# A recurrent graph stage: the next groups' x copied a round ahead, and the tail of a round moved over other slots

## The reference, cut to what matters

```python
A = (adj != 0).astype(x.dtype)
h = x
for l in range(weight.shape[0]):
    m = jnp.einsum('bnd,de->bne', h, weight[l])
    agg = jnp.einsum('bij,bid->bjd', A, m)
    h = _gru_cell(agg, h, w_ih, w_hh, b_ih, b_hh)
return h * mask[..., None]
...
x = _layernorm(x + _L2_gnn_ref(x, adj, nodemask, ...), axis=-1)
```

## Time and profile before

| | |
|---|---|
| median of 3 runs | 1141.59 us (1139.44 to 1142.74) |
| the profiled execution | 1139.14 us, span 1137.3 us |
| mean granted TensorE clock | 0.967 of full speed |
| TensorE matmuls | 998.3 us busy, 88% of the span |
| VectorE | 901.4 us, 79% |
| ScalarE | 770.9 us, 68% |
| GpSimd | 725.5 us, 64% |
| chain that ended last | TensorE 57%, VectorE 19%, ScalarE 9% |

### The profile page before, as it was taken

The page is one execution under the profiler, slowest core; times in us unless marked ns, Lnnn a source line. Parts: engine busy times, 40 slices in busy tenths (PEclk is TensorE's granted clock), DMA queues, the critical chain, the costliest instruction groups (busy, mean ns, idle before and its releaser), DMA issues.

```text
span 1137.3 us, 21302 instructions
## 1 busy us (share of the span) xinstructions
PE 998.3 (88%) x6138; PEld 602.2 (53%) x6138; DVE 901.4 (79%) x2511; ACT 770.9 (68%) x1311; POOL 725.5 (64%) x751
## 2 busy tenths in 40 slices
PE   3699998495989998998998999899899999958884
PEld 2599998242344544454454454445445445547663
DVE  4599999373679878977977987897797798778996
ACT  1388887473667777776776777777677677726664
POOL 0589898293458657656855865765685685565553
PEclk9699999698999999999999999999999999979997
DMA  6133331234443432333333233242333333303323
GB/s 164 54 105 107 106 110 52 61 64 67 52 71 62 74 75 46 79 60 65 74 64 73 56 74 74 46 83 55 65 80 59 74 56 59 64 11 82 89 75 82
DMA packets 261150, 81.59 MB, mean 72 GB/s; under 512 B 188499, under 2 KB 260972, under 8 KB 261100
## 3 DMA queue, kind: packets, MB, share of 16 engines
q1 hardware_dynamic: 247274, 80.15, 32.3%
q10 hardware_dynamic: 13826, 0.85, 0.9%
HBM read 28.58 MB, written 8.81 MB: 33 GB/s over the span
## 4 chain that ended last, share of the span: by engine, by line
PE 57%; DVE 19%; ACT 9%; issue 7%; POOL 3%; ACTq 2%; DMA 1%; DVEq 0%; SPq 0%; POOLq 0%
PE psum L1198 15%; PE psum L1193 15%; PE psum L1194 15%; PE psum L1222 6%; DVE st L816 4%; DVE x L827 2%; PE psum L1281 2%; ACT psum L727 2%; DVE mv L820 2%; ACT rt L749 2%; DVE ws L963 2%; ACTq L703 2%; PE psum L1236 2%; DVE ot L1105 2%; PE psum L1296 1%
## 5 line engine op out<-in xcount | busy, mean ns | idle before, releaser
L587 POOL TENSOR_TENSOR zh<-zw,ht 128x512 f32<-128x512 f32 x160 | 203.6, 1272 | 102.5 <-ACT zw L752 80.6
L560 POOL TENSOR_TENSOR htp<-ht,htp 128x512 f16<-128x512 f32 x128 | 149.1, 1165 | 117.2 <-ACT htp L738 117.2
L1193 PE MATMUL psum<-htp,wh_hi 128*128 128x512 f16 x480 | 182.6, 380 | 39.3 <-ACT rt L749 24.9
L1193 PE MATMUL psum<-pth,wx_hi 128*128 128x512 f16 x480 | 183.3, 382 | 13.8 <-ACT pth L712 13.6
L1198 PE MATMUL psum<-ptl,wx_hi 128*128 128x512 f16 x480 | 183.3, 382 | 4.1 <-DVE ptl L1012 3.2
L1194 PE MATMUL psum<-pth,wx_lo 128*128 128x512 f16 x480 | 183.2, 382 | 0.0
L1198 PE MATMUL psum<-htp,wh_hi 128*128 128x512 f16 x480 | 182.4, 380 | 0.0
L1194 PE MATMUL psum<-htp,wh_lo 128*128 128x512 f16 x480 | 182.4, 380 | 0.0
L752 ACT ACTIVATE zw<-psum,brz,unscale 128x512 f32<-128x512 f32 x160 | 124.4, 777 | 67.2 <-PE psum L1198 67.2
L993 DVE SCALAR_TENSOR_TENSOR rt<-psum,bhn,rt 128x512 f32<-128x512 f32 x160 | 119.6, 748 | 57.8 <-ACT rt L749 55.7
L712 ACT ACTIVATE pth<-psum 128x512 f16<-128x512 f32 x160 | 95.6, 597 | 93.1 <-PE psum L1222 77.3
(11 more groups left out here) (162 smaller groups left out, 1844.4 us busy)
## 6 DMA issues: line engine op xcount, KB each, us to landing
adj<-in_adj_dram SPq DMA_DIRECT2D x32, 256.0 KB, 2.9
x<-in_x_dram SPq DMA_DIRECT2D x32, 256.0 KB, 3.3
adjr<-in_adj_dram SPq DMA_DIRECT2D x32, 256.0 KB, 3.0
out_dram<-yo SPq DMA_DIRECT2D x8, 768.0 KB
hnp<-htp SPq DMA_TRANSPOSE x128, 3.1
out_dram<-xq SPq DMA_DIRECT2D x32, 50.0 KB
v<-in_L_gnn_W_dram SPq DMA_DIRECT2D x2, 640.0 KB, 5.3
x3q<-x SPq DMA_DIRECT2D x16, 50.0 KB
```

The costliest lines, as they stand in the source:

```text
L560: nc.gpsimd.tensor_tensor(HT_LO[s % 2], HT[s][:, :], HT_HI[s % 2], ALU.subtract).then_inc(b_htl, 1)
L587: nc.gpsimd.tensor_tensor(ZH[s % 2][:, :], ZW[s % 2][:, :], HT[s][:, :], ALU.mult).then_inc(b_zh, 1)
L1193: mm(dst, w_h[:, col:col + P], h[:, :], start=start, stop=False)
```

## The change

- **x pair.** For l = 0 each stream has a buffer of its own for the pair (`X_OF`): s = 0 and 1 two new ones (`HXP`), made 16 and 15 slots ahead by ScalarE and VectorE (slots 4, 5 and 5, 6 of the round before), s = 2 and 3 the buffers `HNP`, made at lags -1 and 0. ScalarE's copy moves behind `HT_HI` and waits for P matmuls of long before instead of N matmuls. The waits for `b_hn` and `b_h0` move to SyncE, ahead of the transposing DMA.
- **A16** moves from lag 0 to lag -2, and its place in VectorE's slot from before q to after q and the low half of x. The loads of adj for s = 2 and 3 are issued a slot earlier.
- **The tail.** Residual add from lag 6 to 9, behind ZH in GpSimd's slot; `bn_stats` from 7 to 10; `bn_aggr` from 8 to 13; `rstd` from 9 to 15; normalisation from 11 to two halves at 16 and 20. On VectorE all of these move from the end of the slot to between A16 and t1.
- **TensorE.** The fp32 transposes move from before Z to between Z and N.
- Stage B begins 16 slots early and ends at lag 20 instead of 11; slots without an item are empty.

```diff
--- before.py
+++ after.py
@@ -52,6 +52,7 @@
...
     TURN = STREAMS * L
+    EARLY, LAST_LAG = 16, 20
     GC = 16
@@ -178,8 +179,9 @@
...
         HNP = [sb(f"hnp{p}", [P, 2 * G4 * D], F16, scope=sbb) for p in range(2)]
+        HXP = [sb(f"hxp{p}", [P, 2 * G4 * D], F16, scope=sbb) for p in range(2)]
         HT_HI, HT_LO = [t[:, 0:G4 * N] for t in HTP], [t[:, G4 * N:2 * G4 * N] for t in HTP]
-        HN_HI, HN_LO = [t[:, 0:G4 * D] for t in HNP], [t[:, G4 * D:2 * G4 * D] for t in HNP]
+        X_OF = [HXP[0], HXP[1], HNP[0], HNP[1]]
         PT_HI = [sb(f"pth{p}", [P, G4 * N], F16, scope=sbb) for p in range(2)]
@@ -301,14 +303,14 @@
...
                     slot(lambda lag: item(j - lag, it))
-            body(0, range(TURN))
+            body(0, range(-EARLY, TURN))
             if unrolled:
...
                     body(it, range(TURN))
-            body(ROUNDS - 1, range(TURN + 11))
+            body(ROUNDS - 1, range(TURN + LAST_LAG))

@@ -334,6 +336,11 @@
...
                 eng.wait_ge(signal, value)
+
+        def halves(t):
+
+            w = G4 * D
+            return t[:, 0:w], t[:, w:2 * w]

@@ -444,20 +451,23 @@
...
             def slot_b(at):
+                x = at(-1)
+                if x and x[0] == 0 and x[1] < 2:
+                    sp.wait_ge(b_a16, gth(x))
+                    load_b(x[1] + 2, x[2])
                 x = at(0)
...
                 p = s % 2
-                if l == 0 and s < 2:
-                    sp.wait_ge(b_a16, gth(x))
-                    load_b(s + 2, it)
                 if l == 2 and s < 2 and not (isinstance(it, int) and it == ROUNDS - 1):
...
                     sp.wait_ge(b_sxl, gth(x))
-                    sp.dma_start_transpose(blocks(HTP[p]), HNP[p][:, :]).then_inc(b_tr[p], 16)
+                    reach(sp, b_hn, nth(x) - 2)
+                    reach(sp, b_h0, gth(x) - 2)
+                    sp.dma_start_transpose(blocks(HTP[p]), X_OF[s][:, :]).then_inc(b_tr[p], 16)
                 else:
@@ -558,11 +568,6 @@
...
                     nc.gpsimd.tensor_tensor(HT_LO[s % 2], HT[s][:, :], HT_HI[s % 2], ALU.subtract).then_inc(b_htl, 1)
-                x = at(6)
-                if x and x[0] == L - 1:
-                    l, s, it = x
-                    wait_apart(pool, b_ym, gth(x))
-                    nc.gpsimd.tensor_tensor(YB[s][:, :], YB[s][:, :], of_group(x2, x), ALU.add).then_inc(b_y, 1)
                 x = at(1)
@@ -588,6 +593,11 @@
...
                 x = at(9)
+                if x and x[0] == L - 1:
+                    l, s, it = x
+                    wait_apart(pool, b_ym, gth(x))
+                    nc.gpsimd.tensor_tensor(YB[s][:, :], YB[s][:, :], of_group(x2, x), ALU.add).then_inc(b_y, 1)
+                x = at(15)
                 if x and x[0] == L - 1:
@@ -710,14 +720,6 @@
...
                     nc.scalar.activation(PT_HI[s % 2][:, :], P_B, ACT.Copy, scale=UP_P / UP_H).then_inc(b_ph, 1)
-                x = at(0)
-                if x and x[0] == 0:
-                    l, s, it = x
-                    reach(act, b_hn, nth(x) - 2)
-                    reach(act, b_tr[s % 2], turned(x) - 16)
-                    if s >= 2:
-                        act.wait_ge(b_h0, gth(x) - 2)
-                    nc.scalar.activation(HN_HI[s % 2], of_group(x2, x), ACT.Copy, scale=UP_H).then_inc(b_sxh, 1)
                 x = at(3)
@@ -736,6 +738,13 @@
...
                     nc.scalar.activation(HT_HI[s % 2], HT[s][:, :], ACT.Copy).then_inc(b_hth, 1)
+                for lag, some in ((-16, (0, 1)), (-1, (2, 3))):
+                    x = at(lag)
+                    if x and x[0] == 0 and x[1] in some:
+                        l, s, it = x
+                        reach(act, b_at, nth(x) - (TURN if s < 2 else STREAMS))
+                        nc.scalar.activation(halves(X_OF[s])[0], of_group(x2, x), ACT.Copy, scale=UP_H)\
+                          .then_inc(b_sxh, 1)
                 x = at(4)
@@ -971,20 +980,53 @@
...
             def slot_b(at):
-                x = at(0)
+                x = at(4)
+                if x:
+                    l, s, it = x
+                    dve.wait_ge(b_z, nth(x))
+                    dve.wait_ge(b_n, nth(x))
+                    nc.vector.scalar_tensor_tensor(C_B, ZW[s % 2][:, :], 1.0, C_B, ALU.subtract, ALU.mult)\
+                      .then_inc(b_q, 1)
+                for lag, some in ((-15, (0, 1)), (0, (2, 3))):
+                    x = at(lag)
+                    if x and x[0] == 0 and x[1] in some:
+                        l, s, it = x
+                        hi, lo = halves(X_OF[s])
+                        dve.wait_ge(b_sxh, gth(x))
+                        nc.vector.scalar_tensor_tensor(lo, of_group(x2, x), UP_H, hi, ALU.mult, ALU.subtract)\
+                          .then_inc(b_sxl, 1)
+                x = at(-2)
                 if x and x[0] == 0:
...
                       .then_inc(b_a16, 1)
-                x = at(4)
-                if x:
-                    l, s, it = x
-                    dve.wait_ge(b_z, nth(x))
-                    dve.wait_ge(b_n, nth(x))
-                    nc.vector.scalar_tensor_tensor(C_B, ZW[s % 2][:, :], 1.0, C_B, ALU.subtract, ALU.mult)\
-                      .then_inc(b_q, 1)
+                x = at(13)
+                if x and x[0] == L - 1:
+                    l, s, it = x
+                    wait_apart(dve, b_bs, gth(x))
+                    for i in range(G4):
+                        last = nc.vector.bn_aggr(MVB[s][:, 2 * i:2 * i + 2], STB[s][:, 6 * i:6 * i + 6])
+                    last.then_inc(b_mv, 1)
+                x = at(10)
+                if x and x[0] == L - 1:
+                    l, s, it = x
+                    wait_apart(dve, b_y, gth(x))
+                    for i in range(G4):
+                        last = nc.vector.bn_stats(STB[s][:, 6 * i:6 * i + 6], cols(YB[s], i))
+                    last.then_inc(b_bs, 1)
+                for lag, some in ((16, (0, 1)), (20, (2, 3))):
+                    x = at(lag)
+                    if x and x[0] == L - 1:
+                        l, s, it = x
+                        wait_apart(dve, b_rs, gth(x))
+                        for i in some:
+                            last = nc.vector.tensor_scalar(
+                                x2[:, bass.ds(it * (STREAMS * G4 * D) + (s * G4 + i) * D, D)], cols(YB[s], i),
+                                MVB[s][:, 2 * i:2 * i + 1], RSB[s][:, i:i + 1], ALU.subtract, ALU.mult)
+                        if lag == 20:
+                            last.then_inc(b_x3, 1)
                 x = at(3)
@@ -1011,35 +1053,6 @@
...
                                                    ALU.mult, ALU.subtract).then_inc(b_pl, 1)
-                x = at(8)
-                if x and x[0] == L - 1:
-                    l, s, it = x
-                    wait_apart(dve, b_bs, gth(x))
-                    for i in range(G4):
-                        last = nc.vector.bn_aggr(MVB[s][:, 2 * i:2 * i + 2], STB[s][:, 6 * i:6 * i + 6])
-                    last.then_inc(b_mv, 1)
-                x = at(0)
-                if x and x[0] == 0:
-                    l, s, it = x
-                    dve.wait_ge(b_sxh, gth(x))
-                    nc.vector.scalar_tensor_tensor(HN_LO[s % 2], of_group(x2, x), UP_H, HN_HI[s % 2],
-                                                   ALU.mult, ALU.subtract).then_inc(b_sxl, 1)
-                x = at(7)
-                if x and x[0] == L - 1:
-                    l, s, it = x
-                    wait_apart(dve, b_y, gth(x))
-                    for i in range(G4):
-                        last = nc.vector.bn_stats(STB[s][:, 6 * i:6 * i + 6], cols(YB[s], i))
-                    last.then_inc(b_bs, 1)
-                x = at(11)
-                if x and x[0] == L - 1:
-                    l, s, it = x
-                    wait_apart(dve, b_rs, gth(x))
-                    for i in range(G4):
-                        last = nc.vector.tensor_scalar(
-                            x2[:, bass.ds(it * (STREAMS * G4 * D) + (s * G4 + i) * D, D)], cols(YB[s], i),
-                            MVB[s][:, 2 * i:2 * i + 1], RSB[s][:, i:i + 1], ALU.subtract, ALU.mult)
-                    last.then_inc(b_x3, 1)
             run_b(dve, slot_b)
@@ -1217,7 +1230,7 @@
...
                     reach(pe, b_pl, n - 1)
-                    for h, half in enumerate((HN_HI[p], HN_LO[p])):
+                    for h, half in enumerate(halves(X_OF[s] if l == 0 else HNP[p])):
                         for i in range(G4):
@@ -1227,6 +1240,11 @@
...
                     support(0)
+                if x:
+                    g = l * GATE
+                    reach(pe, b_z, n - 1)
+                    hi_passes(Z_B, wh_hi, wh_lo, P, HT_HI[p], True)
+                    lo_pass(Z_B, wh_hi, P, HT_LO[p], False)
                 y = at(4)
@@ -1236,10 +1254,6 @@
...
                 if x:
-                    g = l * GATE
-                    reach(pe, b_z, n - 1)
```

(19 more changed lines are left out.)

1 line of the change is left out of this document (removed).

## The result

The changed kernel takes 1488.38 us (median of 4 runs, 1487.35 to 1488.54) where the kernel before took 1141.37: a ratio of 1.304, 95% interval [1.302, 1.306]. The forecast of the direction and its mechanism held. The time, 1416, was 72 us too low, and the range ended at 1470.

What follows compares the result with a forecast made beforehand. It took a plain slot, 4.33 us, to be bound by TensorE. 118 + 112 + 39 - 5 + 5 + 5 = 274 us on 1139.1 made 1413, with 2.5 for the median 1416; range 1375 to 1470.

Steps and rivals of the forecast that it cites:

- Direction and mechanism: Slower, chance 0.94: VectorE's steps moved ahead of T1 wait for their inputs and delay T1, which TensorE waits for.
- The three waits: On VectorE: statistics on GpSimd's add, normalisation on the inverse deviation, 28 times some 4 us each; A16 on P matmuls, 2.5.
- Statistics: Slots 6 to 9: VectorE waits for GpSimd's residual add behind ZH; 28 slots grow by 4.2 us, 118 us.
- Normalisation: Slots 12 to 15: VectorE waits for the inverse deviation behind ZH; 28 slots grow by 4.0 us, 112 us.
- Change of round: Slots 18 to 3: A16's wait for P matmuls and the moved transposes cost 12.7 us each; net 39 us more.
- A16 held by GpSimd: Slots 18, 19, 0 and 1: A16 also stands while ZH runs on GpSimd; 39 us with it, 10 without.
- Low half of x: On VectorE, moved before T1: costs nothing, as its input is a slot old and idle time covers it.
- The rest: X copies in slots 4 and 5, 3 us; normalisations beside HT_LO in slots 16 and 17, 2; start 1; end 4.
- Relief: Change of round: ScalarE's wait for the N matmuls goes, 5.06 us a round at most.
- rival (3): Each of 56 long waits lowers TensorE's clock for seven matmuls, 1.5 us each, 84 in all: 1500; chance 0.12.

Runs made afterwards that it cites:

- e1: The changed kernel with the residual add at lag 8 and the inverse deviation at lag 14, one slot earlier each; 1214.09 us.
- e2: The changed kernel with A16 at lag -1 instead of -2, nothing else; 1415.35 us.
- e10: The changed kernel with A16 still at lag -2, but at the end of VectorE's slot, behind PT_LO; 1416.41 us.
- e11: The changed kernel with all its lags, but statistics, aggregation and normalisation at the end of VectorE's slot, behind PT_LO; 1200.80 us.
- e3: The changed kernel with residual add at lag 8, inverse deviation at lag 14 and A16 at lag -1; 1150.51 us.
- e4: The changed kernel with 12 more matmuls, result unused, on TensorE between Z and N in slots 6 to 9 and 12 to 15; 1417.13 us.
- e8: e3 with statistics, aggregation and normalisation at the end of VectorE's slot, behind PT_LO; 1119.43 us.
- e9: The kernel before with the x pair's change (high halves at lags -10, -2; low -8, 0), transposes behind Z, normalisation at lag 12; 1110.64 us.
- e5: The kernel before with the x pair's part of the change alone; A16, tail and transposes as before; 1121.23 us.

## Why the prediction was wrong, point by point

- **Direction and mechanism**: right. The three waits are the three longest of VectorE, 28 times in the rounds each, and e1, e2, e10 and e11 take them away one by one. Undoing both kinds (e3) gives back 338 of the 347 us that the change cost.
- **Statistics**, 118 us: at full clock (e4) slots 6 to 9 take 8.1 + 3 x 8.47 = 33.5 us, 4.05 each above plain, 113 in all. Right. The first is 0.4 shorter because its ZH starts at +0.68 instead of +1.06.
- **Normalisation**, 112: 33.7 in e4, 4.09 each, 115 in all. Right.
- **Change of round**, 12.7 each: in e4 slots 18 and 19 take 14.3 - 8.7 = 5.6 us above plain ones (forecast 6.0), and slots 0 to 3 take 23.7 - 17.3 = 6.4 (forecast 6.7): 12.0. Right.
- **A16 held by GpSimd**: right. It took 1.31 us and ended 0.27 us behind ZH.
- **Low half of x**, costed at nothing as its input is a slot old: wrong, though small here. In the changed kernel the two early ones take 1.12 us instead of 0.69, and in e8 slot 6, with no other new step ahead of t1, is 0.29 us longer than a plain one. Beside GpSimd's HT_LO for its whole length it takes 1.62 us (e9). The Trainium skill's page "SBUF — State Buffer", section "SBUF: two separate sides", names beside the two-port mode also a VectorE instruction with two SBUF inputs as bound by the shared ports, against a GpSimd one that reads SBUF. The trace of e9 agrees: the low half reads two SBUF tiles, and it took 1.62 us beside HT_LO, which reads two as well.
- **The rest**: slots 4 and 5, with the x copies on ScalarE, cost 1.1 us a round instead of 0.4. Two normalisations beside HT_LO in slots 16 and 17 cost 0.9 us a round at full clock (e4), 6 us in all instead of 2. The start is 1.5 us later and the last stage 4.0 us longer, as forecast. That the filled kernel, at 1417.13, meets the forecast of 1416 so closely is in part luck: these small errors, of 3 to 5 us each, go both ways.
- **Relief**, 5.06 us a round at most: 3.9 seen in e5, 4.9 in e10. The new place of the transposes and SyncE's two waits had no run of their own; e10 has both, and its 4.9 leaves 0.2 us a round for them.
- **The clock**: here the prediction failed. The mechanism stood there as rival (3), with its price of 1.5 us for each wait, and it came true: in slots 7 to 9 and 12 to 15 of all seven rounds, in slot 6 of rounds 1 and 7 and in slot 18 of rounds 1 to 6. These are 57 stretches, 1.25 us each, 71 us. The step that failed is the choice of value: between a pause of 0.9 us that kept full clock and one of 6.8 that lost it, a pause of 3.3 was given no cost in the sum and 0.12 of the chances, and the range took in only two thirds of the price. 1416 + 71 = 1487, against 1488 measured. The trace of before also held pauses between the two ends, which the prediction did not use. In the last stage TensorE paused twice for 2.70 us ahead of the same instruction: the granted clock stayed at 1.00 after the one and was 0.50 from 1.2 us behind the other's end on:

```profile
1060.54 0.64 PE L1264 MATMUL psum<-ident,ot 128*100 128x128 f32 x4 [2.70 <-DVE ot L1105]
...
1089.18 0.64 PE L1264 MATMUL psum<-ident,ot 128*100 128x128 f32 x4 [2.70 <-DVE ot L1105]
```

```profile
1060.00:1065.00 5.00, 4.28 (x27) 3.68 (x28) 4.70 (x23) 3.34 (x6) 1.63 (x3) 1.00 0.19 51
...
1090.50:1093.50 3.00, 3.00 (x14) 2.81 (x13) 2.63 (x16) 1.88 (x4) 1.05 (x2) 0.50 0.03 8
```

So a fall behind 3.3 us was at least as likely as not, the middle of the two ends (1458) was the value to take, and the range had to reach the upper one, 1500. The sign that the prediction set for this, a granted clock below 0.9 in rounds 1 to 7, was also too coarse: it is 0.90 there, with 71 us lost.

## What to carry to other kernels

With software slots, "one slot of slack" means nothing until both places within the slots are known: a user that stands early in its engine's slot still waits for a source that stands late in the slot before. Put steps with slack at the end of the slot, behind the ones that the bottleneck waits for, and look which other engine's full-size steps run there. And if a wait idles TensorE as long as a pause in the trace behind which the clock fell, were it only once, price the clock in the sum and not beside it.
